# Experts' maxima spread over two batches, a bank copied ahead of the expert's blocks, and the last group's products in another order

## The reference

```
h        = gelu(x @ W1 + b1)             # 512 x 2048, exact gelu
shared   = h @ W2 + b2                   # 512 x 384
expert   = h @ We[index] + be[index]     # 512 x 128
out      = x + concat(shared, expert)    # 512 x 512
```

## Time and profile before

| | us |
|---|---|
| median of 3 runs (1277.38 to 1280.73) | 1279.31 |
| the profiled execution | 1280.58 |
| its span | 1278.8 |
| TensorE, busy share | 95% |
| VectorE, busy share | 83% |
| ScalarE, busy share | 60% |
| granted TensorE clock, mean | 0.983 |

### The profile page before, as it was taken

How to read it: one execution, slowest core, us unless ns; L and a number is a source line. 1 busy time by engine, 2 the same in 40 slices (tenths; PEclk the granted TensorE clock), 3 DMA queues, 4 the chain that set the end, 5 groups by cost and what they waited for, 6 DMA issues and landing times.

```text
span 1278.8 us, 26299 instructions
## 1 busy us (share of the span) xinstructions
PE 1218.9 (95%) x10284; PEld 1007.6 (79%) x10284; DVE 1062.9 (83%) x1426; ACT 769.1 (60%) x1026; POOL 4.6 (0%) x12
## 2 busy tenths in 40 slices
PE   9998579999899999999999999999999999999997
PEld 4455345778788888888888888888888888888885
DVE  7986467788788889888888889888898988989875
ACT  4665234666665756666575666756667566666651
POOL 0000000000000000000000000000000000000000
PEclk9999889999999999999999999999999999999998
DMA  7232421101112021021202112120120203002100
GB/s 271 91 133 94 169 102 71 59 34 49 52 67 67 33 88 44 33 66 66 66 33 73 59 33 66 44 87 34 44 88 33 66 34 99 33 33 94 39 35 34
DMA packets 38833, 86.78 MB, mean 68 GB/s; under 512 B 5872, under 2 KB 6128, under 8 KB 36208
## 3 DMA queue, kind: packets, MB, share of 16 engines
q1 hardware_dynamic: 37616, 77.63, 18.0%
q0 software_dynamic: 1152, 8.39, 1.8%
HBM read 69.22 MB, written 16.78 MB: 67 GB/s over the span
## 4 chain that ended last, share of the span: by engine, by line
PE 56%; DVE 25%; issue 7%; DMA 6%; ACT 4%; SPq 1%; DVEq 0%; ACTq 0%; POOL 0%; POOLq 0%
PE banks L1577 9%; PE banks L1579 9%; PE banks L1578 9%; PE q_ps L1577 5%; PE q_ps L1578 5%; PE q_ps L1579 5%; DVE h_ring L925 5%; PE out_ps L1577 4%; PE out_ps L1578 4%; PE out_ps L1579 4%; DMA t_sum<-we_dram 3%; DVE x_lo L925 3%; DVE x_max L911 2%; DMA h_ring<-we_dram 2%; DVE u L1205 1%
## 5 line engine op out<-in xcount | busy, mean ns | idle before, releaser
L1577 PE MATMUL banks<-x_hi,w_hi 128*128 128x256 f16 (+1 forms) x1704 | 469.5, 276 | 33.9 <-ACT kept L705 12.4
L1579 PE MATMUL banks<-x_hi,w_lo 128*128 128x256 f16 (+1 forms) x1704 | 469.5, 276 | 0.0
L1578 PE MATMUL banks<-x_lo,w_hi 128*128 128x256 f16 (+1 forms) x1704 | 469.4, 275 | 0.0
L925 DVE SCALAR_TENSOR_TENSOR h_ring<-u,scale,h_ring 128x1536 f16<-128x1536 f32 (+1 forms) x120 | 253.7, 2114 | 22.0 <-ACT h_ring L595 15.8
L1577 PEld LDWEIGHTS banks<-x_hi,w_hi 128*128 128x128 f16 x1704 | 167.0, 98 | 74.5 <-ACT kept L705 16.1
L1578 PEld LDWEIGHTS banks<-x_lo,w_hi 128*128 128x128 f16 x1704 | 167.1, 98 | 27.1 <-issue 0.6
L1579 PEld LDWEIGHTS banks<-x_hi,w_lo 128*128 128x128 f16 x1704 | 167.1, 98 | 22.8
L705 ACT ACTIVATE kept<-banks 128x512 f32<-128x512 f32 x180 | 105.9, 588 | 130.7 <-PE banks L1579 130.7
L737 ACT ACTIVATE u<-u,b_sb,undo 128x512 f32<-128x512 f32 x120 | 91.1, 806 | 96.2 <-DVE u L1211 96.2
L1577 PE MATMUL q_ps<-h_ring,w_hi 128*128 128x256 f16 (+1 forms) x504 | 146.1, 290 | 0.0
L1578 PE MATMUL q_ps<-h_ring,w_hi 128*128 128x256 f16 (+1 forms) x504 | 145.8, 289 | 0.0
(11 more groups left out here) (181 smaller groups left out, 2128.0 us busy)
## 6 DMA issues: line engine op xcount, KB each, us to landing
out_dram<-x_raw SPq DMA_DIRECT2D x63, 256.0 KB, 2.4
x_raw<-x_dram SPq DMA_DIRECT2D x60, 256.0 KB, 4.0
t_sum<-w2o_dram SPq DMA_DIRECT2D x26, 512.0 KB, 3.7
t_sum<-we_dram SPq DMA_DIRECT2D x26, 512.0 KB, 4.3
h_ring<-we_dram POOLq DMA_DIRECT2D x8, 1024.0 KB, 5.1
h_ring<-w_dram SPq DMA_DIRECT2D x5, 1024.0 KB, 7.2
e_raw<-we_dram SPq DMA_DIRECT2D x3, 1024.0 KB, 4.9
t_sum<-w2p_dram SPq DMA_DIRECT2D x2, 1024.0 KB, 4.9
```

What stands on the lines that cost most here:

```text
L925: return nc.vector.scalar_tensor_tensor(to, of, s, hi, ALU.mult, ALU.subtract)
L1577: nc.tensor.matmul(ps, hi, v_hi, start=start, stop=False, skip_group_check=True)
L1578: nc.tensor.matmul(ps, hi, v_lo, start=False, stop=False, skip_group_check=True)
L1579: return nc.tensor.matmul(ps, lo, v_hi, start=False, stop=stop, skip_group_check=True)
```

## The change

1. VectorE takes the experts' maxima one at a time: 0 after c12(1, 0), 1 after c12(1, 1), 2 after c22(1, 2), 3 after c12(1, 2), 4 in the last group of batch 1, 5 at its end, 6 early in batch 2, 7 before c12(2, 0).
2. At the start of a full batch ScalarE makes the third copy of bank A ahead of `eh_split` and `ht_split`, and VectorE takes c22 ahead of `eh_split`; `add_es(b, 0)` moves behind c12 (also in batch 3).
3. `take_p1` is cut in two: `take_c11` (both additions to c11, with a semaphore of its own) and the rest.
4. TensorE's last group follows a table of its own, `TAIL`, with four units of H blocks first; the tail's operations on VectorE and the stores are put in a matching order.

```
@@ tables
+TAIL = ((0, P1, 0), (0, P2, 0), (1, P1, 0), (1, P2, 0), (1, P4, 0), (1, P5, 0), (0, P6, 0), (0, P5, 0),
+        (0, P7, 0), (0, P4, 0), (1, P7, 1), (1, P6, 1), (1, P7, 0), (1, P6, 0), (1, P3, 0), (0, P3, 0))
@@ SP, the tail
-            for o in (2, 1, 3):
+            for o in (1, 2, 3):
                 store(B - 1, 1, o)
@@ ScalarE, full_batch
                 keep(b, 0, 1)
+                keep(b, 0, 2)
                 eh_split(b, 0)
                 ht_split(b - 1, 1 - par, 3)
-                keep(b, 0, 2)
@@ VectorE
-                nc.vector.tensor_tensor(c2, c2, kept_xy[:, KEPT_A], ALU.add).then_inc(r_mixed, 1)
-
-            def take_p1(b, par):
-                k, (c11, c12, c2), un = b - FULL, r_tiles(par), undo2[:, par, 1:2]
+                nc.vector.tensor_tensor(c2, c2, kept_xy[:, KEPT_A], ALU.add).then_inc(p45_added, 1)
+
+            def take_c11(b, par):
+                k, c11, un = b - FULL, r_tiles(par)[0], undo2[:, par, 1:2]
                 dve.wait_ge(r_summed, k + 1)
                 dve.wait_ge(residual_done, b + 1)
-                nc.vector.scalar_tensor_tensor(c11, heads[:, 1], un, c11, ALU.mult, ALU.add).then_inc(r_mixed, 1)
+                nc.vector.scalar_tensor_tensor(c11, heads[:, 1], un, c11, ALU.mult, ALU.add).then_inc(r_heads, 1)
+                dve.wait_ge(r_heads, k + 1)
+                nc.vector.scalar_tensor_tensor(c11, heads[:, 0], un, c11, ALU.mult, ALU.add)
+
+            def take_p1(b, par):
+                k = b - FULL
                 dve.wait_ge(xy_taken, 2 * k + 2)
-                nc.vector.scalar_tensor_tensor(kept_xy[:, 5], heads[:, 0], un, kept_xy[:, 5], ALU.mult, ALU.add
-                                               ).then_inc(r_mixed, 1)
-                dve.wait_ge(r_mixed, 5 * k + 2)
-                nc.vector.scalar_tensor_tensor(c11, heads[:, 0], un, c11, ALU.mult, ALU.add).then_inc(r_taken, 1)
+                nc.vector.scalar_tensor_tensor(kept_xy[:, 5], heads[:, 0], undo2[:, par, 1:2], kept_xy[:, 5],
+                                               ALU.mult, ALU.add).then_inc(r_taken, 1)
...
@@ VectorE, full_batch
                 add_ht(b - 1, 3)
+                c22(b, 0)
                 eh_split(b, 0)
-                if not first_full(b):
-                    add_es(b, 0)
-                c22(b, 0)
                 ht_split(b - 1, 3, 1 - par)
-                if first_full(b):
-                    add_es(b, 0)
                 c12(b, 0)
+                add_es(b, 0)
...
                 if sure:
+                    take_c11(b - 1, 1 - par)
                     take_p1(b - 1, 1 - par)
@@ VectorE, batch (w2_s is batch 2, sums is batch 1)
                 if w2_s:
-                    all_e_tops_of(7)
+                    all_e_tops_of(6)
...
                     w2_s_split(0)
+                    all_e_tops_of(7)
                 c12(b, 0)
+                if sums:
+                    all_e_tops_of(0)
...
                 if sums:
-                    all_e_tops_of(0, 1)
+                    all_e_tops_of(1)
...
                 c22(b, 2)
+                if sums:
+                    all_e_tops_of(2)
...
                 c12(b, 2)
                 if sums:
-                    all_e_tops_of(2, 3, 4)
+                    all_e_tops_of(3)
...
                 ht_split(b, 2, par)
+                if sums:
+                    all_e_tops_of(4)
...
-                    all_e_tops_of(5, 6)
+                    all_e_tops_of(5)
@@ VectorE, the tail
             ht_split(B - 1, 3, 1)
+            mix(B - 1, 1, 0)
+            take_c11(B - 1, 1)
             take_xy(B - 1, 1, False)
-            mix(B - 1, 1, 0)
             add_p45(B - 1, 1)
+            mix(B - 1, 1, 1)
+            mix(B - 1, 1, 2)
+            mix_c12(B - 1, 1)
             take_xy(B - 1, 1, True)
-            mix(B - 1, 1, 1)
             take_p1(B - 1, 1)
             add_u2(B - 1, 1)
             add_u3(B - 1, 1)
-            mix(B - 1, 1, 2)
-            mix_c12(B - 1, 1)
             take_p3(B - 1, 1)
             mix(B - 1, 1, 3)
@@ TensorE
-            for unit in range(len(ODD)):
-                layer2(B - 1, D - 1, unit)
+            for unit in range(len(TAIL)):
+                full_unit(B - 1, D - 1, unit, TAIL)
```

More of the change, by code:

```diff
@@ L159, in build @@
         late_x_tops = xy[:, 0, 0:2]
+        heads = out_ps[:, 0].rearrange("p (j n) -> p j n", j=2)
         x_loaded = [sem("x_loaded_even"), sem("x_loaded_odd")]
@@ L253, in build @@
         r_taken = sem("r_taken")
+        r_heads = sem("r_heads")
+        p45_added = sem("p45_added")
         r_mixed = sem("r_mixed")
@@ L1297, in add_p45 @@
                 dve.wait_ge(xy_taken, 2 * k + 1)
[L1298 to L1302 removed]
+                nc.vector.tensor_tensor(c2, c2, kept_xy[:, KEPT_A], ALU.add).then_inc(p45_added, 1)
+            def take_c11(b, par):
+                k, c11, un = b - FULL, r_tiles(par)[0], undo2[:, par, 1:2]
                 dve.wait_ge(r_summed, k + 1)
                 dve.wait_ge(residual_done, b + 1)
[L1305 to L1306 removed]
+                nc.vector.scalar_tensor_tensor(c11, heads[:, 1], un, c11, ALU.mult, ALU.add).then_inc(r_heads, 1)
[3 more added lines that the diff above has]
+                k = b - FULL
                 dve.wait_ge(xy_taken, 2 * k + 2)
[L1308 to L1311 removed]
+                nc.vector.scalar_tensor_tensor(kept_xy[:, 5], heads[:, 0], undo2[:, par, 1:2], kept_xy[:, 5],
+                                               ALU.mult, ALU.add).then_inc(r_taken, 1)
             def add_u2(b, par):
                 k = b - FULL
[L1316 removed]
+                dve.wait_ge(p45_added, k + 1)
+                dve.wait_ge(r_taken, k + 1)
                 nc.vector.tensor_tensor(kept_xy[:, KEPT_57], kept_xy[:, KEPT_57], two(kept_xy[:, 5:6]), ALU.add
@@ L1322, in add_u3 @@
                 k, (c11, c12, c2) = b - FULL, r_tiles(par)
-                dve.wait_ge(r_mixed, 5 * k + 4)
+                dve.wait_ge(r_mixed, 2 * k + 1)
                 nc.vector.tensor_tensor(c2, c2, two(kept_xy[:, 4:5]), ALU.add).then_inc(out_ready[2], 1)
@@ L1329, in take_p3 @@
                 dve.wait_ge(q_summed, 4 * (b - PLAIN) + 4)
-                dve.wait_ge(r_taken, k + 1)
-                dve.wait_ge(r_mixed, 5 * k + 5)
+                dve.wait_ge(r_mixed, 2 * k + 2)
                 nc.vector.scalar_tensor_tensor(c12, q_ps[:, 3, 1], undo2[:, par, 1:2], c12, ALU.mult, ALU.add
@@ L1734, in mixed_unit @@
                 else:
-                    ps, opens = out_ps[:, 0].rearrange("p (j n) -> p j n", j=2)[:, 0 if i == P1 else 1], d == 0 and i == P1
+                    ps, opens = heads[:, 0 if i == P1 else 1], d == 0 and i == P1
                     if opens:
@@ L1770, in mixed_unit, with full_unit @@
                 return done
-            def full_unit(b, d, unit):
-                units = ODD if d % 2 else EVEN
+            def full_unit(b, d, unit, units):
                 pair, i, back = units[unit]
-                if unit == (2 if d % 2 else 0):
+                of_h = [n for n, (_, p, _) in enumerate(units) if p in (P1, P2, P3)]
+                of_t = [n for n, (_, p, _) in enumerate(units) if p not in (P1, P2, P3)]
+                if unit == of_h[0]:
                     pe.wait_ge(h_lo_done, D * b + d + 1)
-                if unit == (0 if d % 2 else 4):
+                if unit == of_t[0]:
                     pe.wait_ge(ht_lo_done, D * (b - PLAIN) + d + 1)
@@ L1785, in layer2 @@
                 if full(b):
-                    return full_unit(b, d, unit)
+                    return full_unit(b, d, unit, ODD if d % 2 else EVEN)
                 if plain(b):
```

## The result

| | before | after |
|---|---|---|
| median of the runs, us | 1278.43 (1277.38 to 1280.73, 4 runs) | 1234.08 (1231.52 to 1235.42, 4 runs) |
| the profiled execution, us | 1280.58 | 1231.52 |
| its span, us | 1278.8 | 1229.7 |
| its granted TensorE clock, mean | 0.983 | 0.997 |

The ratio is 0.9648 with a 95% interval from 0.9627 to 0.967: faster by 44.4 us in the medians and by 49.1 us in the two profiled executions. The forecast was 1233.0.

What follows compares the result with a forecast made beforehand. TensorE's work plus its standstills and half-speed stretches bound the kernel. -25.6 - 18 + 3.2 - 6.1 = -46.5 from the profiled 1280.6 us gives 1234.1, with the median 1.3 lower 1233; range 1226 to 1250.

Steps and rivals of the forecast that it cites:

- Part A: Batches 1 and 2: experts' maxima taken one at a time remove early TensorE stalls; -25.6 us, bounds -28 to -18.
- the new stall at the experts' total: End of step (2,0): maximum 7 ends at 179.3 us, TensorE reaches the total at 176.0; 3.3 us stall.
- The 5 us of half clock: Batch 2: two close stalls, at c22(2,0) and the experts' total, bring 5 us at half clock, costing 2.5 us.
- Rival 2: Expert loads 3 and 6 land 2.3 us late each, GpSimd unable to issue beside VectorE; 1238 or 1241 us; chance 0.10.
- Part B: Batches 4 to 15: copy of bank A first and c22 earlier end TensorE's waits at P4 and P3; -18 us.
- the bank's release: Full batches: ScalarE frees bank A at 1116.75, P1(b,1) wants it at 1116.8; no margin, 0.1 us a batch charged.
- rival 1: Full batches: bank A freed late, P1(b,1) waits about 0.9 us a batch; 1244 us; chance 0.13.
- rival 3: Steady part: VectorE is the real pacemaker, stalls come back elsewhere, no gain there; 1251 us; chance 0.06.
- rival 4: Full batches: sums before c11(b,1) and the split behind delay P5 by 4.9 us each; slower, 1292 us; chance 0.03.
- Batch 3: Sums behind c12 delay first gelus, so P1 goes 2.4 us later; with half a half-clock stretch +3.2 us.
- Part C: Tail: H blocks first leave 0.8 us of the wait, no half clock, seven VectorE operations left; -6.1 us.
- a limit between 2.5 and 3.3 us: Half clock follows TensorE standstills: 2.5 us left 2.4 GHz, 3.3 us didn't; batch 3's 3.1 us charged half of 1.7.

Runs made afterwards that it cites:

- experiment 3: Changed kernel with only ScalarE's third copy of bank A put back behind the expert's and T blocks, VectorE as changed: 1246.11 us.
- experiment 7: Changed kernel, batch 3 alone with the third copy behind the blocks and c22 behind the expert's split, sums still behind c12: 1233.71 us.
- experiment 8: Changed kernel with ScalarE's split of S1 behind the first gelus in both halves of batch 3: 1223.15 us.
- experiment 10: Changed kernel with the maximum of batch 2's x ahead of maximum 3: 1230.85 us.
- experiment 2: Changed kernel with the full batches' old order back on ScalarE (third copy) and VectorE (c22, sums), batch 3 included: 1249.96 us.
- experiment 6: Changed kernel, in batch 3 alone the four sums of the expert's first half ahead of c12 again, copy still first: 1232.44 us.
- experiment 9: Changed kernel with maximum 7 ahead of VectorE's half of the split of the W2 sums in batch 2: 1230.31 us.
- experiment 11: Changed kernel with S1's split behind the gelus, maximum 7 ahead of the W2 sums' split and x's maximum ahead of maximum 3: 1217.35 us.
- experiment 12: Changed kernel with S1's split behind the gelus, maximum 7 and x's maximum earlier, batch 2's expert maximum behind c22(2,0): 1217.39 us.

## Why the prediction was right

**The whole.** 1233.0 against a median of 1234.08. Undone one at a time, the parts are worth 23.7, 15.9 and 5.2 us, 44.8 together against the measured 44.4, so as far as these medians can tell they hardly touch each other, and the sum of parts was the right form. That sum leaves nothing for the third edit in batches 3 to 14 (`take_p1` cut in two, forecast at nothing), which no experiment undid alone. The profiled execution was 49.1 us faster, 2.6 us more than the sum of 46.5. It was the fastest of its four, and the one with the highest clock (0.997, the others 0.994 to 0.996). That the medians agree to 1.1 us is partly luck: the forecast took 1.3 us off the profiled time, because the kernel before had its median there, and in the changed kernel the median lies 2.6 us above the profiled time.

**Part A: right, every step within 0.8 us but for the clock.** x's total stood at 141.95 (141.5 forecast), c22(2,0) let TensorE go on at 173.71, after a standstill of 1.9 us (173.3 and 2.0 forecast), the new stall at the experts' total was 3.2 us (3.3), c11(2,1) came at 183.85 (183.5). The 5 us of half clock that I charged there didn't come in the profiled execution, and its 2.5 us are about the difference between -25.6 and -27.8. Four of the nine profiles with the same standstill have a stretch there, of 3.4 us (experiments 3, 7, 8 and 10), and the lower clock of the changed kernel's other executions leaves room for one. The working has two slips that cost nothing. The stalls that it lists sum to 27.6 us and not 28.3; the missing 0.7 is the wait for the gelus in batch 1. And its list of half-clock stretches lacks the one of 326.5 us, at P1(3,3).

**Rival 2, late loads, fell.** VectorE's two waits for expert loads are 5.4 us in total (8 forecast), the issues took 0.53 us beside its splits, and from issue to maximum it was 5.5 and 5.0 us. (The Trainium skill, SBUF — State Buffer, the section on the two separate sides, says that GpSimd can't write a DMA's descriptors while VectorE runs in a 2-port mode. The products with a scalar and a tensor and the sum that ran beside these two issues show no such delay; what a copy would do, no run here shows.)

**Part B: right, and experiments 2 and 3 show the mechanism.** -18.9 against -18: I had charged 0.1 us a batch for the bank's release, and there was no such wait, so rival 1 fell. Rivals 3 and 4 fell with it: VectorE and ScalarE kept pace, and TensorE's only waits left from batch 4 to 15 are four for c11, 1.6 us together, the longest 0.5.

**Batch 3: right in size, by a chain of which I saw half.** The 4.2 us from c12 to P1 were 4.17 us, and P1(3,1) came 2.35 us later against matmul 980 (79.45 us behind it and 77.10), +2.4 forecast. The rest of +3.4 goes with the half-clock stretch behind P1(3,1), which the kernel before didn't have. But my step named only the sums' place behind c12 as the cause. Experiments 2 and 6 show that the blocks' place behind the copy would have held P1(3,1) by itself too, by 1.7 us (gaps of 2.54 and 0.81).

**Part C: right, -5.8 against -6.1.** The wait of 3.30 us became 0.68, 0.84 with the 0.16 (0.8 forecast), the half clock went, and behind the last xy product seven operations were left. (The kernel before had 14 from 1270.38 us on; the prediction counts 15.) In the kernel before the half clock lasted 6.9 us; undoing the tail gave 3.4 us of it. So between profiles the part's price is 4.8 us with the shorter stretch and 5.8 with the longer; the medians have 5.2.

## What to carry to other kernels

Where an engine executes in a fixed order, read a wait twice: who released it, and what that releaser was queued behind. A single load buffer with several loads in a row makes its consumer stand for each of them; put the consumers one at a time into places where the load has had time to land. Before moving an operation back behind another, list everything that feeds the same chain: in batch 3 two moves each held the same gelus, undoing either alone gave nothing that the times could tell, and taking the gelus out of the chain (at P1(3,3) too) gave 10.9 us.

## What the runs showed of the hardware

**The same standstill brought the half clock in one execution and not in the next.** P1(3,1) in the kernel of experiment 9:

```profile
259.39 0.28 PE L1593 MATMUL banks<-x_hi,w_hi 128*128 128x256 f16 x1 [2.91 <-ACT u L734]
```

and in the changed kernel:

```profile
260.11 0.40 PE L1593 MATMUL banks<-x_hi,w_hi 128*128 128x256 f16 x1 [2.91 <-ACT u L734]
```

Idle for 2.91 us both times; the first goes on at 2.4 GHz (0.28 us a matmul), the second at 1.2 GHz (0.40 us) until 262.99. That stretch is 3.4 us long and begins 0.5 us before the wait ends. A longer wait can leave the clock whole where a shorter one doesn't: in the changed kernel there was no stretch at the 3.16 us of the experts' total, while in experiment 2 one followed a wait of 1.99 us:

```profile
711.07 0.28 PE L1596 MATMUL banks<-x_hi,w_hi 128*128 128x256 f16 x1 [1.99 <-ACT kept L712]
```

```profile
712.00:716.00 4.00, 4.00 (x24) 2.84 (x22) 3.57 (x4) 2.00 (x4) 0.00 (x0) 0.57 0.00 0
```

My forecast had put a limit between 2.5 and 3.3 us. Counted over the fourteen profiles, from 120 us on, a stretch began in a standstill or within 1.4 us behind it in none of the 19 with idle times of 1.5 to 1.89 us, in 8 of 19 with 1.9 to 2.7, in 10 of 17 with 2.9 to 3.2, and in all 19 with 3.3 us or more.

**The spread of the runs fits this.** Only the profiled executions show their stretches; of the others the record has the mean clock. The four executions of the changed kernel took 1231.52, 1233.56, 1234.6 and 1235.42 us, at mean clocks of 0.997, 0.996, 0.994 and 0.994. A stretch of 3.4 us at half clock takes 0.5 x 3.4 / 1230 = 0.0014 from the mean and costs at most 1.7 us. So two stretches more would explain 0.997 to 0.994, and up to 3.4 of the 3.1 to 3.9 us. Experiments 11 and 12, whose profiles have no standstill above 2.1 us and no stretch at half clock from 120 us to TensorE's end, spread over 1.3 and 0.6 us. A single thousandth of the mean clock says little: the profile of experiment 12 has 0.999 from a half-clock stretch behind TensorE's last matmul, where it costs nothing. By these numbers a long standstill that is closed is worth its own length and, in some executions, up to 1.7 us more.
